# Four turned-score attentions of a decoder: pairs in a loop against an unrolled pipeline of single sequences

## The reference

```
L0_xattn (X0):    q from x, k and v from the context; scores masked by a 0/1 mask of [seq, query, key]
L2_attn  (SELF2): q, k, v each from a two-layer MLP of x (computed by the stage before, kept in SBUF); no mask
L2_xattn (X2):    q from x, k and v from the context; no mask
L3_attn  (MQA):   one k and v head shared by all, rotary turn of q and k, causal mask
each:  attn = softmax(q k^T / sqrt(8) + mask);  x = layernorm(x + (attn v) Wo + bo)
```

## Time and profile before

| | us |
|---|---|
| three executions: lowest, median, highest | 2082.51, 2086.05, 2087.24 |
| profiled execution: its span | 2082.5 |
| profiled execution: its own time | 2082.51 |
| X0, from the first transpose (L902) to the last normalised tile | 255.35 to 403.4 |
| SELF2, from the first copy of kept q and k to the last normalised tile | 941.91 to 1070.50 |
| X2, from the first transpose (L902) to the last division (L1114) | 1070.76 to 1199.77 |
| MQA, from the first transpose (L902) to the last normalised tile | 1325.60 to 1483.69 |

### The profile page before, as it was taken

How to read it: one execution, slowest core, us unless ns; L and a number is a source line. 1 busy time by engine, 2 the same in 40 slices (tenths; PEclk the granted TensorE clock), 3 DMA queues, 4 the chain that set the end, 5 groups by cost and what they waited for, 6 DMA issues and landing times.

```text
span 2082.5 us, 43945 instructions
## 1 busy us (share of the span) xinstructions
PE 1623.7 (78%) x14747; PEld 1041.4 (50%) x14747; DVE 1232.0 (59%) x3892; ACT 935.4 (45%) x2731; POOL 552.1 (27%) x903
## 2 busy tenths in 40 slices
PE   4555389758778867897778833699799999996997
PEld 3333255435445555454445512456577777763443
DVE  3434556556665746215757678567566666654776
ACT  2222444346665534433434444333366665662433
POOL 2321422212114533101212233222143334431100
PEclk6555599869999988998989955799899999997999
DMA  5000000000000000000020000000000000000000
GB/s 207 2 1 1 0 2 0 0 1 0 0 0 2 2 0 1 0 1 1 0 104 1 0 1 0 1 1 0 1 1 1 0 0 0 0 1 0 0 0 20
DMA packets 2943, 18.47 MB, mean 9 GB/s; under 512 B 1049, under 2 KB 1177, under 8 KB 1561
## 3 DMA queue, kind: packets, MB, share of 16 engines
q1 hardware_dynamic: 2842, 17.17, 2.2%
HBM read 16.06 MB, written 1.05 MB: 8 GB/s over the span
## 4 chain that ended last, share of the span: by engine, by line
PE 58%; issue 15%; DVE 10%; ACT 7%; DVEq 4%; POOL 4%; POOLq 1%; DMA 0%; ACTq 0%; SPq 0%
PE ps L3075 5%; PE ps L936 4%; PE ps L950 3%; PE ps L2640 3%; PE ps L2650 3%; PE ps L2664 3%; PE ps L2619 3%; PE ps L2626 3%; PE ps L1005 2%; PE ps L2484 2%; PE ps L1526 2%; PE ps L358 2%; PE ps L915 2%; PE ps L1013 2%; PE ps L2611 1%
## 5 line engine op out<-in xcount | busy, mean ns | idle before, releaser
L376 POOL TENSOR_TENSOR arena<-arena,C 128x1 f32<-128x1 f32 (+1 forms) x176 | 99.5, 568 | 532.9 <-DVE arena L1131 304.9
L1095 DVE TENSOR_REDUCE arena<-ps 128x4 f32<-128x512 f32 x256 | 164.1, 685 | 88.2 <-PE ps L946 48.3
L2577 POOL TENSOR_TENSOR arena<-arena 128x512 f32<-128x512 f32 x128 | 132.6, 1041 | 233.6 <-DVE arena L2865 233.1
L471 POOL TENSOR_TENSOR arena<-arena,C 128x512 f32<-128x512 f32 x80 | 83.2, 1040 | 356.9 <-ACT arena L672 128.6
L1063 ACT ACTIVATE arena<-ps 128x512 f32<-128x512 f32 x256 | 132.2, 603 | 89.9 <-PE ps L962 89.9
L3075 PE MATMUL ps<-WA,arena 128*128 128x512 f32 x256 | 133.5, 603 | 0.4 <-ACT arena L3099 0.4
L1526 PE MATMUL ps<-hid,WA 128*20 128x16 f32 x1024 | 56.9, 196 | 88.1 <-DVE hid L1577 88.1
L2774 ACT ACTIVATE arena<-ps,arena 128x256 f32<-128x256 f32 x256 | 119.9, 477 | 11.8 <-issue 8.1
L2783 ACT COPY arena<-ps 128x512 f32<-128x512 f32 x128 | 69.1, 589 | 121.6 <-PE ps L2650 121.6
L2857 DVE TENSOR_REDUCE arena<-ps 128x2 f32<-128x512 f32 x128 | 82.4, 686 | 43.8 <-PE ps L2640 42.3
L358 PE MATMUL ps<-bias,ones_b 128*128 128x128 bf16 (+1 forms) x336 | 99.1, 295 | 0.0
(11 more groups left out here) (474 smaller groups left out, 4136.7 us busy)
## 6 DMA issues: line engine op xcount, KB each, us to landing
WA<-w_late SPq DMA_DIRECT2D x1, 4228.0 KB, 13.1
WA<-w_early SPq DMA_DIRECT2D x1, 1600.0 KB
R<-rows SPq DMA_DIRECT2D x1, 1282.0 KB, 7.0
WB<-w_rest SPq DMA_DIRECT2D x1, 1152.0 KB, 11.4
xT_all<-x_T SPq DMA_DIRECT2D x1, 1024.0 KB, 6.4
x_all<-x_tok SPq DMA_DIRECT2D x1, 1024.0 KB, 14.4
arena<-mask SPq DMA_DIRECT2D x1, 1024.0 KB
ctxT_all<-ctx_T SPq DMA_DIRECT2D x1, 1024.0 KB
```

The costliest lines, as they stand in the source:

```text
L1095: red = nc.vector.tensor_reduce(v_(z, ATT, "m", 4 * t, 4), heads(ps[z][t][:, :]), AXX, ALU.max)
L2577: nc.gpsimd.tensor_tensor(p, p, v_(z, LAT, "rec", 4 * u + 2 * x, 2).unsqueeze(2).broadcast_to([128, 2, 256]), ALU.mult).then_inc(l_sub, 1)
```

## The change

All four attentions lose the loop: `att_steps` counts k from -2 to 17 and every engine's work is written out per sequence. The fold is no longer made by VectorE: ScalarE copies the turned maxima to bf16 (`m_rows`), and 16 matmuls of 128 columns with a constant selector `pick_b` (made once at the start) subtract them, for X0, SELF2 and X2 in two halves, two banks ahead of `scores(k+1)` and two behind it. The maxima are turned ahead of scores_T. The copies of x, context, mask and kept q and k into the arena are gone; matmuls and the widening read the originals. y of a sequence is written to the other bank set, its `added` and `normed` come a step later, `scores` waits for `y_read` of n-3, and a stage starts with waits for single sequences.

At the start of the program, on VectorE, and the order of the banks:

```
+            nc.vector.tensor_copy(pick_b[:, :, :], cst("foldmask").unsqueeze(2).broadcast_to([128, 4, 128]))
...
-        WIDE_Q, OT, FOLD, TURN = 0, 512, 1024, 1280
-
-        T_ORDER = (2, 3, 0, 1)
+        WIDE_Q, OT, TURN = 0, 512, 1280
+
+        T_ORDER = (2, 0, 3, 1)
```

POOL, in `satt_pool`:

```
+            for k in att_steps():
+                if sub == S_MQA and has(k + 1):
+                    wides(k + 1)
+                if has(k - 2):
+                    finish(k - 2)
+                if sub != S_MQA and has(k + 2):
+                    wides(k + 2)
```

TensorE, in `satt_pe`: the entry waits, the waits of `scores`, the fold, and the order of a step:

```
+            def entered(n):
+
+                if sub == S_X0:
+                    pe.wait_ge(var_ok, of_run(tail_run[S_LSTM], BATCH - 2 + n))
+                elif sub == S_X2 and n == 1:
+                    pe.wait_ge(y_read, of_run(st_run[S_SELF2], BATCH - 2))
+                elif sub == S_MQA and n == 0:
+                    pe.wait_ge(g_in, BATCH)
+
...
+            def scores(n):
+                z = n % 2
+                pe.wait_ge(q_wide, of_run(st, n))
+                if kind == "kept":
+                    pe.wait_ge(mlp_kept, 3 * (n // MLP_SEQS) + 2)
+                    if n == 1:
+                        pe.wait_ge(mlp_kept, 3 * MLP_GROUPS)
+                else:
+                    pe.wait_ge(v_sb, of_run(a, n))
+                if n == 0:
+                    if sub == S_X2:
+                        pe.wait_ge(y_read, of_run(st_run[S_SELF2], BATCH - 1))
+                elif n == 1:
+                    if sub == S_MQA:
+                        pe.wait_ge(f_var, LIN_STEPS + F1_STEPS + f2_count(BATCH + F2_R - 1))
+                if n > 1:
+                    pe.wait_ge(o_sb, of_run(a, n - 2))
+                if n > 2:
+                    pe.wait_ge(y_read, of_run(st, n - 3))
                 for j in range(4):
...
-            def fold_T(s, t):
-                fold = v_(s, ATT, "P", FOLD, 256).bitcast(BF16)
-                return nc.tensor.matmul(ps[s][t][:, :], ones_b[rows(t), :], fold[rows(t), :], start=False, stop=True,
-                                        skip_group_check=True)
...
+            def fold_T(n, banks):
+                s = n % 2
+                pe.wait_ge(mT_sb, of_run(st, n))
+                for j in range(4):
+                    for t in banks:
+                        mm = nc.tensor.matmul(ps[s][t][:, 128 * j:128 * j + 128], pick_b[rows(t), j, :],
+                                              m_rows[s][rows(t), :], start=False, stop=True, skip_group_check=True)
+                        if j == 3:
+                            mm.then_inc(sT_ps, 1)
+
...
+            early = T_ORDER if sub == S_MQA else T_ORDER[:2]
+            for k in att_steps():
+                if has(k):
+                    maxima_T(k)
+                    scores_T(k)
+                    fold_T(k, early)
+                if has(k + 1):
+                    scores(k + 1)
+                if has(k):
+                    if len(early) < GROUPS:
+                        fold_T(k, T_ORDER[2:])
+                    values(k, T_ORDER[:2])
+                if has(k - 1):
+                    if k == BATCH:
+                        pe.wait_ge(y_read, of_run(st, k - 3))
+                    turned(k - 1)
+                if has(k + 2):
+                    front_x(k + 2)
+                if has(k):
+                    values(k, T_ORDER[2:])
+                if has(k + 2):
+                    front_qk(k + 2)
+                if has(k):
+                    heads_T(k)
+                if has(k + 2):
+                    front_v(k + 2)
+                if has(k - 1):
+                    output(k - 1)
```

ScalarE, in `satt_act`, and VectorE, in `satt_dve`:

```
+            for k in att_steps():
+                s, n = k % 2, k + 2
+                if has(k):
+                    act.wait_ge(mT_ps, of_run(st, k))
+                    nc.scalar.copy(m_rows[s][:, :], ps[(k + 1) % 2][2][:, 0:128]).then_inc(mT_sb, 1)
+                    for m, t in enumerate(T_ORDER):
+                        act.wait_ge(sT_ps, of_run(st, k, GROUPS, m + 1))
+                        nc.scalar.activation(v_(s, ATT, "PT", 512 * t, 512), ps[s][t][:, :], ACT.Exp,
+                                             scale=SCALE).then_inc(pT_sb, 1)
+                if has(n) and kind != "kept":
+                    act.wait_ge(xT_ps, of_run(xt_run[sub], n))
+                if has(k - 1):
+                    act.wait_ge(on_ps, of_run(a, k - 1))
+                    nc.scalar.copy(v_((k - 1) % 2, ATT, "OnT"), ps[s][0][:, 256:384]).then_inc(on_sb, 1)
+                if has(n) and kind != "kept":
+                    nc.scalar.copy(v_(s, ATT, "xcT"), x_part(sub, n)).then_inc(xT_sb, 1)
+                if has(k):
+                    act.wait_ge(oT_ps, of_run(a, k))
+                    nc.scalar.copy(v_(s, ATT, "P", OT, 512), ps[s][2][:, :]).then_inc(oT_sb, 1)
+                if has(n):
+                    if kind == "kept":
+                        act.wait_ge(mlp_kept, 3 * (n // MLP_SEQS) + 3)
+                        v = kept_of(n, 2)
+                    else:
+                        if sub != S_MQA:
+                            act.wait_ge(qkv_ps, of_run(qkv_run[sub], n, 2, 2 if n == 0 else 1))
+                            nc.scalar.copy(qkT_of(s), ps[s][1][:, 0:256]).then_inc(qk_sb, 1)
+                        act.wait_ge(qkv_ps, of_run(qkv_run[sub], n, 2, 2))
+                        if has(k - 1):
+                            act.wait_ge(y_ps, of_run(tail_run[sub], k - 1))
+                        v = v_part(sub, n)
+                    nc.scalar.copy(own_heads(s)[:, :, 0:HD], v.rearrange("p (h d) -> p h d", h=HEADS)).then_inc(v_sb, 1)
...
+            for k in att_steps():
+                if has(k):
+                    cut_up(k)
+                if sub == S_MQA and has(k + 1):
+                    rope(k + 1)
+                if has(k - 1):
+                    divided(k - 1)
+                if has(k - 2):
+                    added(k - 2)
+                if has(k + 1):
+                    maxima(k + 1, 0, 2)
+                if has(k - 2):
+                    normed(k - 2)
+                if has(k + 1):
+                    maxima(k + 1, 2, 4)
 
 
```

More of the change, by code:

```diff
@@ new lines, in has, with att_steps, of_run, own_heads @@
+        def has(n):
+            return 0 <= n < BATCH
+        def att_steps():
+            return range(-2, BATCH + 2)
+        def of_run(run, n, each=1, part=None):
+            return (run * BATCH + n) * each + (each if part is None else part)
+        def own_heads(s):
+            return arena[s][:, VAUG].rearrange("p (h d) -> p h d", h=HEADS)
+        def x_part(sub, n):
+            return ps[0][1][:, 256:384] if sub == S_X2 and n == 0 else ps[n % 2][0][:, 0:128]
+        def v_part(sub, n):
+            return ps[0][1][:, 384:512] if sub == S_X2 and n == 0 else ps[n % 2][0][:, 128:256]
@@ L994, in step @@
-                if before:
-                    output(i, s)
-                pe.wait_ge(m_fold, nth(st, i, s))
-                for t in T_ORDER:
-                    fold_T(s, t).then_inc(sT_ps, 1)
-                if after:
-                    scores(i, s, 1)
-                va = arena[s][:, VAUG].rearrange("p (h d) -> p h d", h=HEADS)
-                for n, t in enumerate(T_ORDER):
-                    pe.wait_ge(pT_sb, nth(a, i, s, GROUPS, n + 1))
+                        nc.tensor.matmul(heads(ps[s][t][:, :]), l,
+                                         ident_b[:, :].unsqueeze(1).broadcast_to([128, 4, 128]), start=False,
+                                         stop=False, skip_group_check=True)
@@ new lines, in turned, with output @@
+            def turned(n):
+                pe.wait_ge(o_sb, of_run(a, n))
+                nc.tensor.transpose(ps[(n + 1) % 2][0][:, 256:384], v_(n % 2, ATT, "O"), ident).then_inc(on_ps, 1)
+            def output(n):
+                pe.wait_ge(on_sb, of_run(a, n))
+                y = ps[(n + 1) % 2][0][:, 384:512]
+                nc.tensor.matmul(y, v_(n % 2, ATT, "OnT"), W[:, name_cols(out_name, out_w, 128)], start=True, stop=False,
+                                 skip_group_check=True)
+                mm = add_bias(y, bias_name, 384, 128) if bias_name else add_bias(y, "self2_out")
+                mm.then_inc(y_ps, 1)
@@ L1160, in last, with added @@
-            def last(i, s):
-                divided(i, s)
-                normed(i, s, -2)
-                added(i, s)
-                moments(s)
-                normed(i, s, -1)
-            if sub == S_MQA:
-                rope(0, 0, 0)
-            maxima(0, 0, 0, 0, 4)
-            in_turn(dve, step, last)
+            def added(n):
+                r = v_(n % 2, ATT, "r")
+                dve.wait_ge(y_ps, of_run(tail_run[sub], n))
+                if has(n + 3):
+                    dve.wait_ge(v_sb, of_run(a, n + 3))
+                nc.vector.tensor_tensor(r, ps[(n + 1) % 2][0][:, 384:512], x_all[:, n, :], ALU.add).then_inc(y_read, 1)
+                dve.drain()
+                stats(dve, n % 2, ATT, r).then_inc(var_ok, 1)
```

300 lines of the change are left out of this document (92 added, 208 removed).

## The result

The changed kernel takes 2019.8 us (median of four runs, 2014.1 to 2022.7) against 2084.6 us before: ratio 0.969, 95% interval 0.967 to 0.971. The forecast was 2036 us. The profiled execution has a span of 2012.3 us against 2082.5, so 70.2 us went where the sum had 49.7. By the medians it is 64.8: both profiled executions were the fastest of their kernel, the changed one 5.7 us under its median and the one before 2.1. The median of 2019.8 lies 0.2 us under the lower end of the forecast's own range, 2020 to 2050, and inside the wider one.

What follows compares the result with a forecast made beforehand. X0 and MQA were taken as nearly TensorE-bound, SELF2 and X2 as bound by a chain through several engines. 39.0 (stages) + 11.0 (entries) + 0.2 (tails) - 0.5 (start) = 49.7 us off 2082.5; median put 3.5 higher: 2036, range 2020 to 2050.

Steps and rivals of the forecast that it cites:

- The fold: All four stages: 16 small matmuls at 34 ns take 0.55 us of TensorE, +0.15 us net per sequence.
- rival C: Fold in all stages: 32-row bf16 matmuls don't overlap, 95 ns each, 2095 us; sign turns at 83 ns; chance 0.08.
- SELF2: SELF2's period: 2.61 to first maxima, 3.02 for reductions and normalisation, 0.61 for cut and hand-over; 6.2 us, gain 1.1.
- X2: X2's period: TensorE's present busy time plus the fold, 6.58 us; taken as 6.6, a gain of 0.85.
- MQA: MQA's period: TensorE's work 8.50 + 0.15 = 8.65 us, with little waiting 8.7; gain 0.5.
- X0: X0's period: TensorE's work 7.98 us plus 0.4 idle from the late fold half, 8.4; gain 0.15.
- rival A: X0, X2 and MQA: late exponentials make each wait 0.3 to 0.4 us longer per sequence, 2051 us; chance 0.17.
- Rival B: SELF2 and X2: VectorE's work ahead of the first maxima makes them 0.75 us late, 2056 us; chance 0.10.
- Rival D: More than forecast: no waiting left, X0 8.1, MQA 8.4, some stage starts at the faster clock, 2019 us; chance 0.05.
- X0's exit and SELF2's entry: Between X0 and SELF2: X0's tail 0.4 us longer, SELF2's entry 1.3 shorter without its copy and part of its idle.
- Entries: Stage starts: TensorE begins sequence 0 earlier; X0 2.5, X2 3.6, MQA 3.6, SELF2 1.3, together 11.0 us less.
- Start: Kernel start: making `pick_b` on VectorE ahead of the recurrence costs +0.5 us (0.2 to 0.9).

Runs made afterwards that it cites:

- Experiment 6: Changed kernel, with VectorE's 128x512 multiply and four wide fold matmuls in place of ScalarE's copy and the selector products: 2020.8 us, 0.9698.
- experiment 3: Changed kernel, with each selector product issued once more on a zero operand, 16 matmuls more per sequence: 2043.7 us, 0.9801.
- Experiment 12: The kernel of experiment 10, with POOL widening q in SELF2 and X2 only behind the cut: 2002.5 us, 0.9608.
- experiment 10: The kernel of experiment 9, with the norm one step later in X2 too and all banks folded early everywhere: 2006.7 us, 0.9630.
- experiment 7: Changed kernel, with all four banks folded ahead of the next scores in every stage, as in MQA: 2019.3 us, 0.9690.
- experiment 1: Kernel before, with only the loops of its four turned-score stages written out, instruction order unchanged: 2079.7 us, 0.9968.
- experiment 8: Changed kernel, with the entries of X0, X2 and MQA put back as before the change: 2030.0 us, 0.9753.
- experiment 9: Changed kernel, with VectorE's multiply, wide fold matmuls and four banks early in X0 and MQA, and SELF2's norm one step later: 2012.4 us, 0.9657.

## Why the prediction was right, and where its size was off

The mechanism and the sign are as forecast; the terms were too small by 20 us together in the profiled execution (16 in the median). By stage the misses are 0.95 (X0), 7.1 (SELF2), 8.3 (X2) and 2.55 us (MQA), and 1.6 between the stages.

*The fold.* Forecast: 0.55 us of TensorE, +0.15 net. Experiment 6 gives the net price against the wide fold as +0.07 in X0, +0.12 in MQA and below zero in SELF2 and X2: the term was right and small, and rival C is ruled out by 23 ns a matmul (experiment 3), where it needed 83 to turn the sign. The Trainium skill's 81 ns per matmul of 128 columns ("TensorE: Matmul & The Clock Gate", Back-to-back issue gap) does not hold for these. The same page (🎯 Why this matters for your kernels) says that matmuls of 32 rows in different row groups run at once; this the runs agree with: 0.16 us for four groups in turn, 0.45 for the same number in pairs.

*SELF2.* The three terms were 2.61 + 3.02 + 0.61 = 6.2; they are 2.32 + 2.74 + 0.71 = 5.77 (982.00 turned maxima, 984.32, 987.06, 987.77). The first is shorter because scores_T is followed after 0.96 us, not 1.07, and because the early half of the fold (forecast 0.28) hides beside the next scores. The second: between the maxima 0.17 us pass for the norm, not the 0.44 us that the earlier trace rows includes. The prediction took those for a normalisation; they are moments, and the change moves them away:

```profile
1007.48 0.18 DVE L1128 BATCH_NORM_AGGREGATE arena<-arena 128x2 f32<-128x6 f32 x1
1007.74 0.15 DVE L1131 TENSOR_SCALAR arena<-arena 128x1 f32<-128x1 f32 x1
```

The third was read too short: from the start of scores_T, which is 0.06 us behind the last maximum, to the cut's end, without the 0.06 us from there to the turned maxima. The cut itself is as long as before, and in both kernels its cast waits for POOL, 0.33 us here; before:

```profile
1001.20 1.04 POOL L471 TENSOR_TENSOR arena<-arena,C 128x512 f32<-128x512 f32 x1
...
1001.95 0.32 DVE L1103 CAST m_cols<-arena 128x16 bf16<-128x16 f32 x1
```

Experiment 12 removes that wait, and SELF2 falls from the 5.64 of experiment 10 to 5.55.

*X2.* This term was off most, by 8.3 us of the 20: "TensorE's present busy time plus the fold, 6.43 + 0.15". Present busy time is not a floor. The turning back shows as 0.66 us long, but where TensorE doesn't wait behind it the next matmul starts 0.49 after its start: the last matmul before each wait adds its way out, some 0.17 us, to the busy time. X2 had three such waits a sequence (who waited for whom, in two sequences: total, times, longest):

```profile
PE ps L1013 <- ACT arena L1066: 0.9, 2, 0.4
PE ps L974 <- ACT arena L1056: 0.7, 2, 0.4
PE ps L936 <- DVE arena L1121: 0.4, 2, 0.3
```

It has none now. My estimate from these numbers is 6.43 + 0.15 - 3 x 0.17 = 6.07; measured are 6.02, all busy. So X2 is bound by TensorE, as the term said, but with less work. The same floor stood in MQA (8.65 forecast, 8.47 measured, all busy).

*X0.* 8.24 against 8.4. No exponential is waited for (rival A is wrong, no idle time in 32.96 us). But the halves are dear in another way: experiment 7 takes 0.34 us off by folding four banks in turn. The forecast charged the halves 0.4 us for lateness. What they cost is 0.34 us of TensorE's own time, with two row groups issued in turn instead of four.

*Rival B* is wrong: VectorE waits 0.78 us ahead of the maxima. *Rival D* came nearest with its 2019 us, partly by luck. Its condition holds: in X0, X2 and MQA TensorE has no waiting left. But it priced only X0 (8.1; 8.24 measured) and MQA (8.4; 8.47), while the extra gain lies in SELF2 and X2. One stage start did meet the faster clock, X2's: its first transpose takes 0.28 us, where the earlier trace rows had 0.48. Still that entry gave 3.1 us and not 4.2.

*What the sum lacked.* The loops (experiment 1): 3 to 5 us. They are no extra to the misses by stage above, which contain them. And the stretch between X0 and SELF2, 4.35 us where X0's exit and SELF2's entry had 0.9: its middle ran the same code in 537.0 us before and 533.8 after. Part of that is the clock: before, four intervals at 1.2 GHz, 13.6 us together, lie between 467 and 567 us, after none. From 470 to 520 us, before, then after:

```profile
470.00:520.00 50.00, 40.50 (x341) 25.62 (x340) 32.17 (x93) 32.49 (x93) 8.93 (x18) 0.92 0.00 0
```

```profile
470.00:520.00 50.00, 38.35 (x343) 23.10 (x341) 34.15 (x97) 33.44 (x97) 8.78 (x18) 1.00 0.00 0
```

Over all fourteen traces this stretch takes 551 to 557 us; what decides it stays open.

*Entries.* Forecast 11.0. Putting three back costs 10 to 13 us (experiment 8; 9.7 forecast for them). X2 and MQA are right (7.6 measured against 8.4, exits included). X0 was forecast at 2.5 and gave nothing against the kernel before: its matmuls met the lower clock for longer, and what was left of the gain TensorE spent on sequence 1. The first transposes of X2 and MQA start 0.05 and 0.40 us behind the start of the last matmul group of the stage before. *Start:* `pick_b` takes 0.34 us of VectorE from its start to the next, not 0.5.

## What to carry over

A tail that the next stage of the pipeline doesn't need may go one step later, and its buffer and its wait must move with it: in SELF2 and X2 taking it back cost 3.08 us a sequence together, where the whole change had gained 2.91, and neither unrolling nor the new arithmetic by itself gave more than 7 us. When a closed chain is costed, add its pieces up from start to start and take out of each total what the change moves away; the busy time of a pipelined engine counts a tail of 0.17 us for each wait and shrinks with them. And look at every engine pair in the new phase: a small VectorE instruction on the path may land inside a long POOL one, and a wait that orders them is then worth more than the overlap.

## What the runs showed of the hardware

- A small cast or subtraction of VectorE in SBUF that starts inside POOL's widening (1.04 us) ends 0.02 to 0.04 us behind it: 0.17 us becomes 0.33, 0.58 or 0.88, and 0.32 in the kernel before. One that starts ahead of the widening takes 0.17 us. The four maxima, which read PSUM, are not held (1.28 us for two, with a widening at 986.39 beside them). The Trainium skill ("SBUF — State Buffer", 🔬 SBUF: two separate sides) has an exclusive lock on a shared pair of ports, held for the whole instruction, between GpSimd and a VectorE instruction with two SBUF inputs or in a 2-port mode. The subtraction has two SBUF inputs, and the trace agrees; whether the cast is in such a mode no run here shows.
- Fold matmuls of 32 rows and float32 scores interleave: the first score matmul, in another row group, starts 0.02 us behind the first two fold matmuls, at 988.91 and 988.89, and the other six start after it. So TensorE doesn't start them in the order of the program.
- When the clock rises at X0's start is not set by the entry alone: 259.4 us before and 263.1 after, but with the entries put back (experiment 8) the first scores take 2.09 us too, and in two kernels with the same X0 code scores_T takes 2.09 us at 264.74 (experiment 9) and 1.14 at 263.81 (experiment 12). What decides it stays open.
